# Splitting all sixteen expert weight parts of the second layer inside its attention

## The reference, cut to what matters

```python
x = x + _L1_gnn_ref(_layernorm(x), adj, L1_gnn_W, L1_gnn_a)      # attention over 64 nodes, then elu
x = x + _L1_ffn_ref(_layernorm(x), L1_ffn_Wg, ..., L1_ffn_W2, L1_ffn_b2)

# in _L1_ffn_ref
gate_logits = x_flat @ Wg + bg + bias
topk_vals, topk_idx = jax.lax.top_k(gate_logits, TOP_K)
h = jax.nn.relu(jnp.einsum('td,edh->teh', x_flat, W1) + b1)      # W1: 8 x 256 x 512
y = jnp.einsum('teh,ehd->ted', h, W2) + b2                       # W2: 8 x 512 x 256
out = jnp.einsum('ted,te->td', y, combine)
```

## Time and profile before

| what | value |
|---|---|
| median of 3 runs | 1402.47 us (1401.55 to 1405.42) |
| the profiled execution's own time | 1402.67 us |
| its span in the profile | 1400.8 us |
| busy: PE, DVE, ACT, POOL | 1061.8, 965.6, 520.3, 784.7 us |
| chain that ended last | PE 55%, issue 16%, DVE 12%, POOL 8%, DMA 4%, ACT 3% |

### The profile page before, as it was taken

How to read it: one execution, slowest core, us unless ns; L and a number is a source line. 1 busy time by engine, 2 the same in 40 slices (tenths; PEclk the granted TensorE clock), 3 DMA queues, 4 the chain that set the end, 5 groups by cost and what they waited for, 6 DMA issues and landing times.

```text
span 1400.8 us, 30856 instructions
## 1 busy us (share of the span) xinstructions
PE 1061.8 (76%) x9022; PEld 875.1 (62%) x9023; DVE 965.6 (69%) x1758; ACT 520.3 (37%) x1067; POOL 784.7 (56%) x807
## 2 busy tenths in 40 slices
PE   5989756379999993667786481679999999999700
PEld 4767545248888882455564370459888888889600
DVE  3788689957777773578896798845555555555377
ACT  2656464802222221457676574012222222222200
POOL 3466755026666645777731375047777777777300
PEclk9999855559999997688888555569999999999955
DMA  9311124015555554333320253012222222223199
GB/s 284 56 46 39 61 95 146 0 30 159 165 165 165 165 143 128 87 112 114 117 61 31 90 171 115 1 57 91 93 91 90 90 91 93 94 90 93 52 356 363
DMA packets 121953, 157.13 MB, mean 112 GB/s; under 512 B 26904, under 2 KB 102176, under 8 KB 121632
## 3 DMA queue, kind: packets, MB, share of 16 engines
q1 hardware_dynamic: 96160, 86.05, 18.9%
q0 software_dynamic: 25728, 70.29, 17.0%
HBM read 95.47 MB, written 60.82 MB: 112 GB/s over the span
## 4 chain that ended last, share of the span: by engine, by line
PE 55%; issue 16%; DVE 12%; POOL 8%; DMA 4%; ACT 3%; SPq 1%; DVEq 0%; POOLq 0%; ACTq 0%
PE bank L814 19%; PE bank L828 19%; PE bank L785 5%; PE bank L797 4%; PE bank L663 4%; POOL WREG L534 3%; DMA arena<-expert_outputs 2%; DVE stats L1090 1%; DVE X L1100 1%; DVE X L1171 1%; SPq L306 1%; PE bank L691 1%; PE bank L681 1%; DVE X L1178 1%; POOL arena L542 1%
## 5 line engine op out<-in xcount | busy, mean ns | idle before, releaser
L605 POOL DMA_INDIRECT arena<-split_tokens,gather_row x272 | 282.0, 1037 | 233.9 <-DVE gather_row L1434 117.9
L1009 ACT ACTIVATE arena<-bank,b1T 128x256 f32<-128x256 f32 (+1 forms) x432 | 167.2, 462 | 497.1 <-PE bank L814 497.1
L828 PE MATMUL bank<-WREG,arena 128*128 x2448 | 289.8, 273 | 11.4 <-issue 5.2
L814 PE MATMUL bank<-arena,WREG 128*128 128x256 f16 (+1 forms) x2592 | 296.3, 269 | 0.0
L828 PEld LDWEIGHTS bank<-WREG,arena 128*128 128x128 f16 x2448 | 235.7, 98 | 47.5 <-issue 19.4
L814 PEld LDWEIGHTS bank<-arena,WREG 128*128 x2592 | 239.9, 99 | 26.5
L1446 DVE CAST arena<-arena 128x512 f16<-128x512 f32 (+1 forms) x136 | 78.7, 578 | 230.9 <-ACT arena L1009 230.9
L614 POOL DMA_INDIRECT expert_outputs<-arena,scatter_row x136 | 155.1, 1141 | 63.9 <-issue 40.6
L663 PE MATMUL bank<-wg_sb,arena 128*128 128x258 f32 x512 | 140.7, 422 | 41.4 <-ACT arena L874 33.6
L534 POOL DMA_INDIRECT WREG<-expert_outputs,pos_i x128 | 125.8, 983 | 61.0 <-issue 38.0
L663 PEld LDWEIGHTS bank<-wg_sb,arena 128*128 128x128 f32 x512 | 101.8, 208 | 65.3 <-issue 37.3
(11 more groups left out here) (190 smaller groups left out, 1343.4 us busy)
## 6 DMA issues: line engine op xcount, KB each, us to landing
expert_outputs<-arena SPq DMA_DIRECT2D x68, 256.0 KB, 2.8
split_tokens<-arena SPq DMA_DIRECT2D x32, 512.0 KB, 2.9
arena<-expert_outputs SPq DMA_DIRECT2D x32, 512.0 KB, 8.0
X<-in_x SPq DMA_DIRECT2D x16, 512.0 KB, 6.0
stage_w<-in_L_ffn_W SPq DMA_DIRECT2D x16, 512.0 KB, 3.4
out<-X SPq DMA_DIRECT2D x16, 512.0 KB, 8.0
arena<-split_tokens,gather_row POOLq DMA_INDIRECT x272
stage_w<-in_L_ffn_w SPq DMA_DIRECT2D x16, 256.0 KB, 2.8
```

Of the source, the lines that this page charges most:

```text
L605: nc.gpsimd.indirect_dma_start(out=gat[:, u * 512:(u + 1) * 512], out_offset=None, in_=table[L], in_offset=bass.IndirectOffsetOnAxis(ap=ga ...
L814: last = mm(hb, w1_at(L, ea, wh, kc, fc), tT[:, tb:tb + width], start=n == 0, stop=n == 3 * KC - 1)
L828: last = mm(ob[a], hsrc[:, h0:h0 + P], w2_at(L, e[a % len(e)], wh, fc), start=fc == 0 and n == 0, stop=fc == FC - 1 and n == 2)
L1009: ins = A(hid[:, h0:h0 + width], bank[2 + 2 * (u % 2) + fc // 2][:, b0:b0 + width], ACT.Gelu if L == 0 else ACT.Relu, bias=cut(b1T, ea * F ...
```

## The change

The tables `HIGH_AT` and `LOW_AT` say which parts are taken in which group of layer 1's attention. ACT does the first half of a group's parts where its one part stood and the second half behind `exp_of_rows(g, 3)`. POOL does parts 0 to 6 behind the gathers of groups 4 to 7, and 7 to 15 behind those. SP issues all 16 loads before it waits for the end of the attention's edges. The three loops beside the routing are gone. For the upper parts ACT waits until `combined[0]` stands at 64.

```diff
+HIGH_AT = ((0,), (1, 2), (3, 4), (5, 6), (7,), (), (8, 9, 10, 11), (12, 13, 14, 15))
+LOW_AT = ((), (), (), (), (0,), (1, 2), (3, 4), (5, 6))
@@ SP
                     else:
-                        load_weights(g // 2, g % 2)
-                if L == 1:
-                    for k in range(2):
-                        load_weights(E // 2, k)
+                        for p in HIGH_AT[g]:
+                            load_weights(p // 2, p % 2)
...
-                if L == 1:
-                    with sp.Fori(E // 2 + 1, E) as e:
-                        for k in range(2):
-                            load_weights(e, k)
@@ POOL
-                        if g >= 3:
-                            low_part((g - 3) // 2, (g - 3) % 2)
-                    for g in range(GROUPS - 3, GROUPS):
-                        low_part(g // 2, g % 2)
+                        for p in LOW_AT[g]:
+                            low_part(p // 2, p % 2)
+                    for p in range(LOW_AT[-1][-1] + 1, 2 * E):
+                        low_part(p // 2, p % 2)
...
-                if L == 1:
-                    with pool.Fori(E // 2, E) as e:
-                        for k in range(2):
-                            stage, hi, lo = weight_parts(L, e, k)
-                            loop_wait(pool, high_ready[L], at(e * 2 + k + 1))
-                            nc.gpsimd.tensor_tensor(lo, stage, hi, ALU.subtract).then_inc(split_done[L], 1)
@@ ACT
                 act.wait_ge(weights_loaded[k][L], e * 16 + 16)
+                if e >= E // 2:
+                    act.wait_ge(combined[0], at(TILES))
...
                     exp_of_rows(L, g, 1)
                     if n < GROUPS and L == 1:
                         diagonal(L, n)
-                    if L == 1:
-                        high_part(L, g // 2, g % 2)
+                    parts = HIGH_AT[g] if L == 1 else ()
+                    half = (len(parts) + 1) // 2
+                    for p in parts[:half]:
+                        high_part(L, p // 2, p % 2)
                     exp_of_rows(L, g, 2)
                     exp_of_rows(L, g, 3)
+                    for p in parts[half:]:
+                        high_part(L, p // 2, p % 2)
...
-                if L == 1:
-                    with act.Fori(E // 2, E) as e:
-                        for k in range(2):
-                            stage, hi, _ = weight_parts(L, e, k)
-                            loop_wait(act, weights_loaded[k][L], e * 16 + 16)
-                            A(hi, stage, ACT.Copy, scale=WSCALE)
-                            A(stage, stage, ACT.Copy, scale=WSCALE).then_inc(high_ready[L], 1)
```

## The result

The changed kernel took 1419.0 us (median of 4 runs, 1416.93 to 1420.74) against 1403.66 us of the kernel before on the same chip: a ratio of 1.0109, 95% interval 1.0091 to 1.0127. It is slower, by 15.3 us; 14.4 had been forecast. The profiled execution took 1419.24 us with a span of 1417.4, which is 16.6 us over the 1400.8 of before.

A forecast was written before the change was run, and what follows sets the result against it. It took DVE, held up by POOL's subtractions, to bound layer 1's routing, and closely matched DVE and ACT paths the attention. Attention +24.7 and routing −10.3 us gave +14.4 on 1402.67: 1417 us, range 1407 to 1424.

The forecast's parts named there:

- Step 1: Layer 1's routing: eight low parts of POOL leave it and no longer hold up DVE; −10.26 us.
- rival E: Locks only move with POOL's work, eight times 1.28 us each way, or other losses stay small: about 1403; chance 0.07.
- Step 2: Attention group 1: ACT's part 2 waits for part 0's buffer; group 2's exponent moves from 643.55 to 652.4 us.
- Step 3: Attention groups 2 to 4: second ACT parts, paired POOL low parts; with group 1's wait, group 5's exponent +15.7 us.
- Rival C: Attention: PE's clock falls too after the buffer wait, 4.8 us over two groups: 1422; chance 0.13.
- A: All steps as summed, attention +24.7 and routing −10.3 us: 1417; chance 0.63.
- Step 4: Attention group 5, left without an ACT part: only 0.59 us of waiting returns, −0.6 us.
- Step 5: Attention groups 6 and 7, four upper parts each: +4.5 and 0.5 us in group 6, +4.6 in group 7.
- The sum: All steps together: +24.7 us in the attention, −10.3 in the routing, +14.4 on 1402.67 us.
- Rival B: Attention: POOL's locks meet idle or one-input DVE instructions, −7 us: 1410; chance 0.12.
- Rival D: Part 2's buffer is ready before ACT asks, later parts fill ACT's waits, attention −10 us: 1392; chance 0.05.

The follow-up runs named there:

- e1: The changed kernel with each low part of POOL one group sooner: 1407.45 us, ratio 1.003 to the kernel before.
- e2: The changed kernel with zeros written in place of POOL's subtraction, layer 1's low weight halves left out: 1402.08 us, ratio 0.9999 to the kernel before.
- e3: The changed kernel with its upper eight parts back beside the routing, the lower eight as changed: 1415.75 us, ratio 1.0099 to the kernel before.
- e4: The kernel before with the lower eight parts moved ahead of the attention on ACT and DVE, upper eight still beside the routing: 1395.52 us, ratio 0.9954.
- e6: e4 with parts 8 to 11 on DVE in groups 6 and 7, DVE forming lower low halves from raw stage: ratios 0.9832 and 0.9898 to the kernel before.

## Why the prediction was right, step by step

The forecast was 1417 and the range 1407 to 1424; 1419.0 was measured. The main steps, the freed routing, the buffer wait and the crowded groups 6 and 7, held to within 1 us each. The losses of groups 2, 4 and 5 were forecast 6.0 us too small, and that the total is still within 2 us is in part luck: see the sum below. Step by step, against the windows above:

- *Step 1, the routing.* −10.26 predicted, −10.13 measured. The price of 1.28 us for each low part, which the prediction takes from it, is too small: two of the eight had run before the window opens at 848.21, while DVE waited for PE and a store.

```profile
841.93 4.21 POOL L594 TENSOR_TENSOR WREG<-stage_w,WREG 128x1024 f32 x2
```

  The other six cost 1.7 us each. At that price rival E's lock, taken eight times in the attention, would be 13.7 us against 10.3 and no draw.
- *Step 2, the buffer of part 2.* The group was to take 652.4 − 618.7 = 33.7 us; it took 33.28, with ACT waiting 7.55 us. e1 took the wait away and the group came back to 26.3.
- *Step 3, groups 2 to 4.* Predicted 28.1, 28.8 and 27.4 us, measured 29.58, 28.25 and 30.88. Part 3's wait and the adds under the low parts of groups 3 and 4 are where they were put (6.61 and 7.48 us for 3.36: +3.3 and +4.1). In group 2 the step counted only the wait; L1108 was held there as well, until 669.23, and in e2, where it was not, the group took 26.07 us although part 3 still waited 3.21. The step also let DVE get something in between two low parts. It got nothing: in both sets a single add took the whole hold, 3.7 us where POOL had begun 0.8 us ahead of the adds and 4.6 us where it had not. The two groups of eight adds, with the shortest, the median and the longest one in ns:

```profile
L1087 DVE SCALAR_TENSOR_TENSOR X<-WREG,cols,X x8: 470/478/3709, 690.3 to 696.4; 128x256 f32<-128x256 f32 x8
L1087 DVE SCALAR_TENSOR_TENSOR X<-WREG,cols,X x8: 474/479/4586, 714.0 to 721.0; 128x256 f32<-128x256 f32 x8
```

  What the step missed most is group 4: low part 7, which I had counted as before, fell on the second set of adds (5.29, +1.9). In e3 it missed them (3.36), and the group took 28.76 us. Counted from the group's exponent POOL began it at 16.9 us in the changed kernel and at 17.6 in e3: 0.7 us decided that, so its place is chance and not design.
- *Rival C, the clock,* was right in part, on top of A and not in its place. After 10.35 us of idle PE's L679 in group 4 took twice as long, and the edges behind it too:

```profile
730.73 2.05 PE L679 MATMUL bank<-arena 128*128 128x256 f32 x4 [10.35 <-DVE X L1158]
```

  Against 1.03 us for four of them at 2.4 GHz, 2.05 is the lower level, 1.2 GHz; the 0.41 us each of the prediction's row lies between the two, so its 16 are a mix of both. Group 4's granted clock is 0.78 where the kernel before had 0.86. What it cost is little: from `add_relu` (729.90) to the next exponent the group took 9.23 us, where e3's group 4 took 8.55 and group 5 of the kernel before 8.50. So some 0.7 us there, not the 2.4 of the rival. L679 took 2.04 and 2.05 us after the waits of groups 2 and 3 too; what that cost was not separated.
- *Step 4, group 5.* −0.6 predicted, +0.4 measured. The window has no part and no lock. The same group took 23.94 us in e2, 24.19 in e3 and 24.21 in e1, at granted clocks of 0.93, 0.93 and 0.86, against 24.84 at 0.86 here, so the mean clock alone does not settle it. The rows do for the 0.65 us against e3: PE's edges ran longer at the lower level. The changed kernel, then e3:

```profile
757.72 1.92 PE L658 MATMUL bank<-b_bc,same_graph 128*128 128x512 f32 x2
759.43 1.60 PE L659 MATMUL bank<-b_bc,ident 128*128 128x512 f32 x2
...
756.94 1.80 PE L672 MATMUL bank<-b_bc,same_graph 128*128 128x512 f32 x2
758.57 1.02 PE L673 MATMUL bank<-b_bc,ident 128*128 128x512 f32 x2
```

  This was only compared, not tested by itself.
- *Step 5, groups 6 and 7.* +4.5 and, with the 0.5, +5.1 predicted; +4.1 and +4.4 measured. The lower bounds, which let half of it hide, are out.
- *The sum.* 24.7 predicted for the attention, 28.6 measured: 3.9 us too little. Two things that no step foresaw took 1.9 of it back, the 1.6 us earlier start and the 0.3 us behind the routing, and the steps' own errors partly cancel (group 3 came out 0.5 us shorter than forecast, groups 6 and 7 together 1.1). With more samples the kernel before also stands at 1403.66 us and not at the 1402.67 that the sum starts from.

*Rival B*, that locks fall where they do no harm, did not come true in the changed kernel. e1 shows how much the place matters: the same subtractions, moved, left the adds of groups 2 to 5 alone and hit the scores instead. *Rival D* named the right place, the buffer of part 2, and e1 met its condition (part 0 split by 626.1 us); it was still slower than before, so D's other half, that later parts fill ACT's waits, is wrong: groups 1 to 4 took 109.7 us in e1 against 102.3 before, and its groups 6 and 7 lost over 4 us each, not 2. *Rival E* fell with group 1.

## What to carry to other kernels

Before moving work into a stage, look for the instruction of each engine that waits there and what it waits for: a second use of a double buffer is only as early as the last user of the first, however idle the engine is that asks. Count the shared path too: a POOL subtraction costs DVE up to its whole length wherever DVE has two-input work (4.1 us for two of 2.1 under the adds, 1.7 for one of 2.1 on average in the routing), so moving it pays only into a wait of DVE, or if DVE does it itself in that wait (e4, e6). And a stage that gains 10 us can be paid for in full by another (e3): compare both windows before taking the gain as one.

## What had not been expected of the hardware

- One DVE instruction is held over two POOL instructions that follow each other at once: the small L1108 (3.79 us), one of the eight adds (4.59 us), in e1 one L1137 (4.98 us). The prediction had DVE slip in between.
- By the profile's start times it is not always the first to start that goes first. In the changed kernel this L1165 starts 0.38 us ahead of POOL's low part (642.21 to 644.35) and still ends only after it; in e1 L1137 starts 0.21 us ahead and is held for both low parts. How exact these starts are was not tested.

```profile
641.83 3.07 DVE L1165 SCALAR_TENSOR_TENSOR X<-arena,X 128x512 f32<-128x512 f32 x1
```

- Chips differ. On two of those met here the kernel before takes 1574 to 1593 us instead of 1402, with a spread of about 2% between runs, and every kernel profiled there shows stops that nothing in the profile releases, up to 20 us in e6.
